# Graph layers: gathers written out one by one, with resident row numbers, and held to the sums eight pairs back instead of four

## The reference, cut to what matters

```python
def _L1_gnn_ref(input_feature, edge_index, edge_attr, W, b, root, We, be, gamma, beta):
    row, col = (edge_index[0], edge_index[1])
    deg = jnp.zeros((n,), input_feature.dtype).at[row].add(1.0) + 1.0
    dinv = deg ** (-0.5)
    norm = (dinv[row] * dinv[col])[:, None]
    h = input_feature
    for l in range(L):                       # L = 5
        xl = h @ W[l] + b[l]                 # 256 -> 256 for each node
        ee = edge_attr @ We[l] + be[l]       # 128 -> 256 for each edge
        msg = norm * jax.nn.relu(xl[row] + ee)
        agg = jnp.zeros_like(xl).at[col].add(msg)
        conv = agg + jax.nn.relu(xl + root[l]) / deg[:, None]
        mean = conv.mean(axis=0)
        var = conv.var(axis=0)
        hbn = (conv - mean) * jax.lax.rsqrt(var + BN_EPS) * gamma[l] + beta[l]
        if l < L - 1:
            hbn = jax.nn.relu(hbn)
        h = hbn + h
    return h
```

## Time and profile before

| | us |
|---|---|
| time, median of 3 runs | 4963.84 |
| lowest and highest of them | 4962.71, 4965.28 |
| span of the profiled execution | 5573.0 |
| edge part of the opening layer, in the profile | about 656 |
| edge part of each later layer, in the profile | about 644 |
| between two layers, in the profile | about 50 |

### The profile page before, as it was taken

One profiled execution on the slowest core, in us unless ns is written; L12 is line 12 of the kernel. 1 busy time (PEld: TensorE's weight loads), 2 busy tenths in 40 slices (PEclk: granted clock), 3 DMA queues, 4 the chain that ended last, 5 costly groups with the idle time before them and its releaser, 6 DMA issues. The chain is left out here.

```text
span 5573.0 us, 95773 instructions
## 1 busy us (share of the span) xinstructions
PE 4065.3 (73%) x21956; PEld 3367.6 (60%) x21957; DVE 3070.1 (55%) x7543; ACT 2243.0 (40%) x4904; POOL 2977.3 (53%) x3202
## 2 busy tenths in 40 slices
PE   6888828769997777766767677766667666776588
PEld 4555517668885666656666566665666656666465
DVE  5555576552224555555555555555555555555634
ACT  2111136522223444444444444444444444444311
POOL 3666619623333666646666466664666646666142
PEclk9999959979998999989999899998999989999689
DMA  6676738536554444434444344443444434444332
GB/s 204 210 212 212 209 95 226 154 123 181 178 178 135 125 127 128 127 106 126 128 127 128 107 125 128 130 127 108 126 129 128 127 107 126 130 127 128 104 120 81
DMA packets 391899, 780.01 MB, mean 140 GB/s; under 512 B 175132, under 2 KB 232080, under 8 KB 374567
## 3 DMA queue, kind: packets, MB, share of 16 engines
q1 hardware_dynamic: 244049, 401.10, 23.2%
q0 software_dynamic: 136704, 358.82, 23.0%
q10 hardware_dynamic: 11094, 19.50, 1.3%
HBM read 666.39 MB, written 114.48 MB: 140 GB/s over the span
## 5 line engine op out<-in xcount | busy, mean ns | idle before, releaser
L2172 POOL DMA_INDIRECT g_g<-xl_rows,g_idx x1664 | 1593.0, 957 | 988.5 <-issue 435.6
L2208 PE MATMUL g_b<-g_we,g_ea 128*128 128x256 f32 x4160 | 1218.2, 418 | 867.1 <-DVE g_msg L2303 652.0
L2208 PEld LDWEIGHTS g_b<-g_we,g_ea 128*128 128x128 f32 x4160 | 751.8, 201 | 1065.5 <-DVE g_msg L2303 750.5
L2221 PEld LDWEIGHTS g_b<-g_onehot,g_msg 128*128 128x128 f32 x8320 | 1149.8, 203 | 195.7 <-DVE agg L2324 76.2
L2221 PE MATMUL g_b<-g_onehot,g_msg 128*128 128x128 f32 x8320 | 1183.0, 288 | 83.4 <-ACT g_msg L2285 35.0
L2324 DVE TENSOR_TENSOR agg<-agg,g_b 128x256 f32 x2080 | 871.4, 419 | 585.0 <-issue 214.0
L2285 ACT ACTIVATE g_msg<-g_msg 128x512 f32<-128x512 f32 x1040 | 652.9, 628 | 1102.7 <-DVE g_msg L2303 817.2
L2303 DVE TENSOR_TENSOR g_msg<-g_g,g_b 128x512 f32<-128x512 f32 x1040 | 713.0, 686 | 679.3 <-DMA g_g<-xl_rows,g_idx 301.7
L2172 POOL DMA_INDIRECT g_g<-xl_table,g_idx x416 | 396.8, 954 | 292.2 <-issue 111.2
L546 PE MATMUL sc_pe_h<-ae_h_rows,sc_onehot 128*128 x1664 | 463.8, 426 | 108.3 <-DVE sc_prod L651 103.5
L2265 ACT ACTIVATE g_away<-iota_row,dst_rel 128x128 f32<-128x128 f32 x1040 | 406.2, 391 | 329.5 <-DMA g_g<-xl_table,g_idx 224.4
(11 more groups left out here) (322 smaller groups left out, 3965.4 us busy)
## 6 DMA issues: line engine op xcount, KB each, us to landing
g_ea<-in_ea SPq DMA_DIRECT2D x260, 512.0 KB
ex_w<-in_f_w SPq DMA_DIRECT2D x80, 1024.0 KB
e_rows<-sc_g SPq DMA_DIRECT2D x52, 1088.0 KB
at_g<-e_rows SPq DMA_DIRECT2D x104, 544.0 KB, 4.6
g_g<-xl_rows,g_idx POOLq DMA_INDIRECT x1664
sc_rel<-rel_row ACTq DMA_DIRECT2D x52, 256.0 KB
xl_rows<-g_rows SPq DMA_DIRECT2D x20, 640.0 KB, 3.3
sc_g<-h_table,sc_idx POOLq DMA_INDIRECT x416
```

Source lines behind the costliest of these rows:

```text
L2172: nc.gpsimd.indirect_dma_start(out=g.g[:, j, 0:width], out_offset=None, in_=table[:, :], in_offset=bass.IndirectOffsetOnAxis(ap=g.idx[:, q ...
L2208: last = nc.tensor.matmul(ep[u % EB][:, i * D:(i + 1) * D], g.ea[:, q, (at + i) * P:(at + i + 1) * P], g.we[:], start=True, stop=True)
L2221: last = nc.tensor.matmul(ps[u % (SB // 2)][:, at:at + P], g.msg[:, j, b * P:(b + 1) * P], g.onehot[:, j, :], start=True, stop=True)
```

## The change

The gathers of a layer are written out, all 208 pairs, without a loop on POOL. Each takes its row numbers from its own column of `k.src_all`, so `g.idx`, `number_half` and `g.numbered` are gone, and with them two copies an iteration on DVE. From the ninth pair of a layer on, pair `n` waits for the sums of pair `n - 8`, a constant; in the opening layer the wait for `g.kept` stays, at the same places. PE, ACT and SP keep their programs.

```diff
-WINDOW = 4
...
-def number_half(k, it, q):
...
-    nc.vector.tensor_copy(g.idx[:, q, :], k.src_all[:, bass.ds(it * BODY + q * HALF, HALF)]).then_inc(g.numbered, 1)
...
-            for q in range(2):
-                number_half(k, 0, q)
...
-        def gather(u):
-            for j in (2 * u, 2 * u + 1):
-                q = j // HALF
+        def gather(n):
+
+            for t in (2 * n, 2 * n + 1):
+                j = t % BODY
                 nc.gpsimd.indirect_dma_start(
                     out=g.g[:, j, 0:width], out_offset=None, in_=table[:, :],
-                    in_offset=bass.IndirectOffsetOnAxis(ap=g.idx[:, q, j % HALF:j % HALF + 1], axis=0)
+                    in_offset=bass.IndirectOffsetOnAxis(ap=k.src_all[:, t:t + 1], axis=0)
                 ).then_inc(g.src_in[j], 16)
 
-        for u in range(BODY // 2):
-            if u % (HALF // 2) == 0:
-                pool.wait_ge(g.numbered, l * (2 * ITERS) + u // (HALF // 2) + 1)
-                pool.sem_inc(g.begun, 1)
-            if u >= WINDOW:
-                pool.wait_ge(g.summed, 2 * (u - WINDOW + 1) + BODY)
-                pool.sem_inc(g.begun, 1)
-            gather(u)
-        with pool.Fori(1, ITERS) as it:
-            for u in range(BODY // 2):
-                if u % (HALF // 2) == 0:
-                    pool.wait_ge(g.numbered, it * 2 + l * (2 * ITERS) + u // (HALF // 2) + 1)
-
-                pool.wait_ge(g.summed, it * BODY + 2 * (u - WINDOW + 1) + BODY)
-                if opening and u % (HALF // 2) == 0:
-                    pool.wait_ge(g.kept, it * 2 - 1 + u // (HALF // 2))
-                pool.sem_inc(g.begun, 1)
-                gather(u)
+        for n in range(ET // 2):
+            if n >= BODY // 2:
+                pool.wait_ge(g.summed, 2 * (n - BODY // 2 + 1) + BODY)
+            if opening and n >= BODY // 2 and n % (HALF // 2) == 0:
+                pool.wait_ge(g.kept, (n - BODY // 2) // (HALF // 2) + 1)
+            pool.sem_inc(g.begun, 1)
+            gather(n)
...
                 add_pair(it, u, seen)
-                if u % (HALF // 2) == HALF // 2 - 1:
-                    number_half(k, it + 1, u // (HALF // 2))
-                    if opening:
-                        keep_half(it, u // (HALF // 2))
+                if opening and u % (HALF // 2) == HALF // 2 - 1:
+                    keep_half(it, u // (HALF // 2))
...
-        self.idx, self.ea = sb("idx", [P, 2, HALF], I32), sb("ea", [P, 2, HALF * P])
+        self.ea = sb("ea", [P, 2, HALF * P])
```

More of the change, by code:

```diff
@@ L1754, in load_first_half_tiles @@
         sp.dma_start(g.ea[:, q, :], a["ea128"][:, q * HALF * P:(q + 1) * HALF * P]).then_inc(g.ea_in[q], 16)
-def number_half(k, it, q):
-    nc, g = k.nc, k.gl
-    nc.vector.tensor_copy(g.idx[:, q, :], k.src_all[:, bass.ds(it * BODY + q * HALF, HALF)]).then_inc(g.numbered, 1)
 def graph_first_inputs(k):
@@ L2398, in __init__ @@
         self.stored = [sem(f"stored{i}") for i in range(2)]
-        self.numbered = sem("numbered")
         self.ea_in = [sem(f"ea_in{i}") for i in range(2)]
```

## The result

The changed kernel takes 4879.27 us, median of 4 runs (4876.67 to 4880.57), against 4964.56 us for the kernel before (4962.71 to 4967.23): a ratio of 0.9826, 95% interval 0.9814 to 0.9837. That is 85.3 us less, where I had forecast 34.5 and given 69 as the most that the window could bring. The direction and the range of 4870 to 4985 us held; the time lies outside the forecast's own 4895 to 4954, and the size was off by more than a factor of two.

What follows compares the result with a forecast made beforehand. POOL's rate of gathers was taken as the floor, with its stops above it. From 4963.8 us, 34.5 for the window and 0 for loop, copies and written-out code gave 4929 us; range for 8 in 10: 4870 to 4985.

Steps and rivals of the forecast that it cites:

- The floor: Edge parts of the graph layers: POOL's gathers at 1.25 us each, 520 us a layer, set the least time.
- The mechanism: Waiting for sums eight pairs back, not four, raises slack from 1.4 to 11.4 us, so POOL's stops should go.
- the common pauses: Profile of the graph layers: all engines stand together for 1.9 to 2.9 us, enough to stop POOL at four pairs.
- How many stops a timed run has: Whole program: 690.8 us of profiled stops less 609.2 us found in the profile only leaves 81.6 us.
- The base: Profiled span against timed runs: the 609.2 us between them were read as mostly POOL's stops.
- The share: Graph layers hold 583.5 / 690.8 = 0.84 of the timed runs' stops, 69 us.
- The middle: Gain from the longer window in the graph layers, taken midway between 0 and 69 us: 34.5 us.
- no stops in timed runs: Graph layers: timed runs may lack POOL's stops, so nothing is gained; part of the no-change case, 4956 to 4972 us, chance 0.32.
- The loop, the copies, the written-out code: POOL's loop gone, DVE's two copies an iteration gone, 416 gathers a layer written out: 0 us each.
- run short of instructions: POOL stops in the written-out gathers while code is fetched: slower, 4990 or 5097 us; chance 0.15.
- Not POOL's to remove: Graph layers: a longer window only shifts the pauses, or timed runs have none; gain 0, 4956 to 4972 us, chance 0.32.
- Faster by far: Graph layers: gathers under 1.25 us unprofiled, so timed runs hold more stops; -150 us, 4814 us, chance 0.08.

Runs made afterwards that it cites:

- the second recording: The kernel before, unchanged, profiled once more on another chip: one time of 5000.51 us, span 4998.7 us.
- the small-load kernel: The written-out kernel with a window of four, edge features loaded in eight 128 KB requests an iteration instead of two of 512 KB: 4895.39 us, ratio 0.9783.

## Why the prediction was wrong in its size, step by step

**The floor: right.** POOL needs 1.25 us a gather and 520 us a layer; the layers are 521 to 522 us now, and a gather left out gives back 1.26 us.

**The mechanism: right, its cause only in part.** I had the way from a pair's first gather to its sums at 8.6 us against a window of 10.0, and let the common pauses use up the remaining 1.4 us. But the pauses aren't in the second recording, and where I read POOL as waiting for sums that it wasn't told of, those sums had ended 5.2 us before it went on. In an undisturbed trace the way is 8.7 us in the median and up to 11.5, with 0.8 us from the sums to the gather behind it that I had left out. What lengthens it are mostly gathers beside a load of features; the pairs 0 to 3 of an iteration take 7.6 to 8.3 us even without loads, where the others take 7.0, and that part wasn't tested.

**How many stops a timed run has: right in total, in part by luck, and then thrown away.** The stops of the profile less the 609.2 us gave 81.6 us, and 85.3 were measured. It is the same sum as 5573.0 less all stops, 690.8, which is 4882.2 us, and the changed kernel takes 4879.27. The base held: of the 695.1 us between the two spans, 575 are stops of the graph layers and 100 of the attention part. But it is a small difference of two large figures, from a recording whose pauses stood where a timed run has others, and on the two other chips where both windows ran the same kernel had 124 us to give. I subtracted only the stops of the graph layers, and got 4990 for a span that came out at 4877.9: 107 of the 112 us between were stops of the attention part, which vanished although nothing there was changed.

**The share: wrong.** I gave the graph layers 0.84 of the 81.6 us, because the attention part had 0.16 of the profile's stops. In the second trace that part has 8.2 us over its 0.30 a gather, the changed kernel 7.4. A share of disturbed waits says nothing about where undisturbed ones are. Without this step the upper bound would have been 81.6 and not 69.

**The middle: the step that failed.** Between 0 and 69 us I took 34.5 for the longer window by no row at all; it brought 85.3. Both ends of that range were cases, not sizes: if timed runs stop at all for this reason, a window that is long enough removes every such stop. The traces show that: no wait of POOL between gathers over 0.3 us is left with windows of five, six and eight pairs. The forecast should have been the full sum, 4964 - 82 = 4882 us, with "no stops in timed runs" kept as the rival that it was.

**The loop, the copies, the written-out code: 0, right.** The loop with a window of eight takes 4875.61 us, the changed kernel 4874.10 on another chip and, with a window of six, 4874.37 on the same one. The copies would have had a price, 13 us, had the window stayed at four. The rule of the Trainium skill that a copy on VectorE blocks GpSimd's writing of descriptors (page "SBUF — State Buffer", section "A bandwidth-pool intuition that's wrong (but worth ruling out)") would have shown as 43 us between these kernels, by my working in the prediction; 1.2 to 1.5 us are within their spread. For copies of 8 columns it can be left out. Nor did POOL run short of instructions: no wait in the earlier trace rows's place is longer than 0.3 us but those at a layer's start.

**The rivals.** "Not POOL's to remove" fell with the window of eight in the loop, where the stops are gone. "Faster by far" supposed a gather faster than 1.25 us without the profiler; the span of the changed kernel is its timed length, so it isn't. I wrote that a gain of over 69 us would show the base wrong. It didn't: the bound was too low.

**Open.** What made the pauses in the first recording. Why before takes 4965 us on one chip and 4998 to 5005 on four others: the only recording of it on the first chip is the disturbed one, and that has no landings of gathers. Why a gather takes 5 ns longer in the small-load kernel. And what the other engines add to the way of pairs 0 to 3.

## What to carry to other kernels

A limit on how far one engine may run ahead cost nothing here where it was longer than the longest way round and its signal, and from then on grew dear fast: 85 to 125 us at four pairs, 502 at three. Measure the longest way, not the median one, and give the window that, here five pairs for a median of 3.5. A profile that is 12% longer than the timed runs should be recorded again before anything is read from its waits; if that isn't possible, take the stops off the span of the whole program and not off one part. Where small gathers share the DMA engines with large loads, look at how many of them land late and what waits for them: cutting the load into pieces that follow the work brought most of what a longer window did.

## What the runs showed of the hardware

- A gather of 128 rows of 1 KB takes 1.25 us of POOL from start to start. Without the feature loads it lands 2.8 us after its start in the median. With a load of 512 KB twice an iteration, two places of the ring land after 4.3 and 4.4 us in the median, and the latest gather of the later layers after 4.9.
- From the modelled end of PE's sums to the start of the gather that waits for them it is 0.79 us.
- One recording had common pauses of all engines and a span 12% over the timed runs, in changed and unchanged parts alike; a second recording of the same kernel, on another chip, had none.
- After a wait of 2 us PE's granted clock was 0.57 over the next 3.5 us, and the sums of the pair that was late already took 1.89 us instead of 1.05. That followed 24 of 93 such waits.
